# Three PSUM banks in turn for the edge products of a graph layer, with the sums issued one round later

## What is computed

```python
h = jnp.maximum(_layernorm(x, axis=-1), 0.0)          # x: 12500 x 64
e = jnp.concatenate([h[src], h[dst]], axis=1)         # 200000 edges, sorted by dst
m = jax.nn.relu(e @ W1 + b1) @ W2 + b2                # 128 hidden, 64 out
s = segment_sum(m, dst); cnt = segment_sum(1, dst)
x = x + s / jnp.maximum(cnt, 1.0)[:, None]
```

## Time and profile before

| | |
|---|---|
| median of 3 runs | 2825.12 us (2822.13 to 2827.91) |
| profiled execution | 2839.25 us, span 2837.4 us |
| mean granted TensorE clock | 0.749 of full speed |
| busy: PE / weight loads / DVE / ACT / POOL | 55% / 42% / 50% / 42% / 48% |

### The profile page before, as it was taken

The page is one execution under the profiler, slowest core; times in us unless marked ns, Lnnn a source line. Parts: engine busy times, 40 slices in busy tenths (PEclk is TensorE's granted clock), DMA queues, the critical chain, the costliest instruction groups (busy, mean ns, idle before and its releaser), DMA issues.

```text
span 2837.4 us, 26976 instructions
## 1 busy us (share of the span) xinstructions
PE 1548.3 (55%) x8249; PEld 1183.2 (42%) x8250; DVE 1428.9 (50%) x3051; ACT 1189.8 (42%) x2414; POOL 1372.7 (48%) x1460
## 2 busy tenths in 40 slices
PE   1656565566465564455544555455455545555556
PEld 0545353444344443344433444344344434434444
DVE  3554343343324665456655666456565556655421
ACT  1223343444314544345444454344344444444444
POOL 6345545445555445444554435545544554554553
PEclk6878777788787777677776777767776777776778
DMA  4532222222134656556565566556565665665541
GB/s 90 163 109 60 59 61 59 60 59 58 58 98 144 202 181 189 167 169 200 179 192 154 178 188 200 186 159 183 184 192 168 186 191 174 183 186 157 174 119 43
DMA packets 258990, 408.46 MB, mean 144 GB/s; under 512 B 45128, under 2 KB 118749, under 8 KB 258841
## 3 DMA queue, kind: packets, MB, share of 16 engines
q1 hardware_dynamic: 211845, 312.84, 35.7%
q0 software_dynamic: 46432, 93.61, 12.5%
q10 hardware_dynamic: 564, 0.23, 0.0%
HBM read 388.12 MB, written 18.38 MB: 143 GB/s over the span
## 4 chain that ended last, share of the span: by engine, by line
PE 48%; issue 36%; another core or an unknown queue 9%; DVE 6%; ACT 1%; DMA 0%; DVEq 0%; SPq 0%; ACTq 0%
PE z L1374 16%; PE bank L1401 12%; PE z L1386 10%; DVE g L1153 4%; PE bank L1419 2%; PE bank L1408 2%; PE z L1445 2%; PE bank L1430 1%; PE z L1461 1%; DVE rows_b L936 1%; PE bank L1268 1%; DVE norms L920 1%; PE z L1268 1%; ACT g L812 0%
## 5 line engine op out<-in xcount | busy, mean ns | idle before, releaser
L672 POOL DMA_INDIRECT g<-p_table,src_e x1403 | 1326.1, 945 | 1425.3 <-PE bank L1401 960.5
L1153 DVE SCALAR_TENSOR_TENSOR g<-z,norms,g 128x1024 bf16<-128x1024 f32 (+1 forms) x884 | 1019.1, 1214 | 43.5 <-issue 25.3
L812 ACT ACTIVATE g<-z 128x1024 f32<-128x1024 f32 x182 | 185.6, 1020 | 1468.0 <-remote 1153.5
L1100 DVE TENSOR_TENSOR acc<-acc,bank 65x128 f32 x191 | 54.2, 284 | 1201.0 <-remote 1069.7
L1374 PE MATMUL z<-work 128*128 128x128 f32 x1464 | 258.8, 348 | 514.2 <-issue 482.9
L1374 PE MATMUL z<-w,work 128*128 128x128 f32 x1438 | 251.9, 345 | 484.3 <-issue 443.8
L1374 PEld LDWEIGHTS z<-work 128*128 128x128 f32 x1464 | 240.3, 256 | 546.0 <-issue 541.7
L1374 PEld LDWEIGHTS z<-w,work 128*128 128x128 f32 x1438 | 234.4, 253 | 512.3 <-issue 509.3
L1401 PE MATMUL bank<-work,g 128*128 128x128 f32 x2902 | 423.4, 307 | 15.4 <-issue 15.1
L1401 PEld LDWEIGHTS bank<-work,g 128*128 128x128 f32 x2902 | 414.1, 227 | 16.8 <-issue 16.7
L1386 PE MATMUL z<-g,ident 128*128 128x512 f32 x726 | 350.8, 605 | 5.8 <-issue 5.7
(11 more groups left out here) (161 smaller groups left out, 1063.6 us busy)
## 6 DMA issues: line engine op xcount, KB each, us to landing
g<-tally_table SPq DMA_DIRECT2D x816, 256.0 KB
rel_q<-rel_table SPq DMA_DIRECT2D x46, 512.0 KB
rows_b<-rel_table SPq DMA_DIRECT2D x45, 512.0 KB
g<-p_table,src_e POOLq DMA_INDIRECT x1403
g<-tally_table SPq DMA_DIRECT2D x68, 128.0 KB
work<-q_table SPq DMA_DIRECT2D x96, 64.0 KB
w<-q_table SPq DMA_DIRECT2D x96, 64.0 KB
g<-p_table SPq DMA_DIRECT2D x12, 512.0 KB
```

The lines of the kernel that those rows point to most:

```text
L672: nc.gpsimd.indirect_dma_start(out=g[:, slot(n), j * HID:(j + 1) * HID], out_offset=None, in_=p_table, in_offset=bass.IndirectOffsetOnAxis ...
L812: nc.scalar.activation(rows_of_p(m), z[:, 0:HID * chunks_in(m)], ACT.Relu).then_inc(r_done, 1)
L1153: nc.vector.scalar_tensor_tensor(product[i % BUFFERS][:, 0:w], turned[:, 0:w], minus_q[:, d:d + 1], tally_row[i % BUFFERS][:, 0:w], ALU.ma ...
```

## The change

`z` becomes three banks used in turn by single quads (`z_of`), in place of a pair used by couples. Identity products and relus signal per quad, and `spread_q` takes one quad. To free a bank, both blocks of sums share one bank, and the first sums of a block wait until the block before is copied. TensorE's round becomes: the first quad's rows of Q of couple m+1, identity products of m, `times_w2`, sums of couple m-1, `dense(m)`, the second quad's rows of Q of couple m+1. The rounds of the other engines keep their order; ScalarE has two relus of 512 columns in place of one of 1024.

```diff
-        u_bank, turn_bank = bank[2:4], bank[4]
+        u_bank, turn_bank = [bank[2][:, 2 * WIN * k:2 * WIN * (k + 1)] for k in range(2)], bank[4]
+        z_of = [bank[0], bank[1], bank[3]]
...
+        def z_quad(n):
+            return z_of[(n - Q0) % len(z_of)][:, 0:HID * chunks_of(n)]
+
+        def quads_to(m):
+            return min(2 * m, QUADS - Q0)
...
             def relu(m):
-                act.wait_ge(z_done, m + 1)
-                nc.scalar.activation(rows_of_p(m), z[:, 0:HID * chunks_in(m)], ACT.Relu).then_inc(r_done, 1)
+                for n in couple(m):
+                    act.wait_ge(z_done, n - Q0 + 1)
+                    nc.scalar.activation(g[:, slot(n), 0:HID * chunks_of(n)], z_quad(n), ACT.Relu).then_inc(r_done, 1)
...
-            def spread_q(m):
-
+            def spread_q(n):
+
+                m, i = couple_of(n), GROUP[n]
                 pe.wait_ge(spread_done, parts_to(m + 1))
-                if m:
-                    pe.wait_ge(r_done, m)
+                if n - Q0 >= len(z_of):
+                    pe.wait_ge(r_done, n - Q0 + 1 - len(z_of))
...
             def sum_edges(m):
 
 
-                pe.wait_ge(r_done, m + 1)
+                pe.wait_ge(r_done, quads_to(m + 1))
                 if m < MEMBER_FROM:
                     pe.wait_ge(m_made, m + 1)
                 k = BLOCK[m]
+                if k and (m == 0 or BLOCK[m - 1] < k):
+                    pe.wait_ge(u_copied, k)
...
             def fast():
-                spread_q(0)
...
+                for n in couple(0):
+                    spread_q(n)
                 for m in range(COUPLES):
+                    if m + 1 < COUPLES:
+                        spread_q(couple(m + 1)[0])
                     add_rows(m)
                     if m >= 2 and m - 2 == BLOCK_END[BLOCK[m - 2]]:
                         times_w2(BLOCK[m - 2])
+                    if m:
+                        sum_edges(m - 1)
                     dense(m)
                     if m + 1 < COUPLES:
-                        spread_q(m + 1)
-                    sum_edges(m)
+                        for n in couple(m + 1)[1:]:
+                            spread_q(n)
                     for i in range(BATCHES):
                         if MEAN_AT[i] == m:
                             turn_batch(i)
+                sum_edges(COUPLES - 1)
```

More of the change, by code:

```diff
@@ L549, in load_window @@
                 if i >= WINDOWS:
-                    sp.wait_ge(zq_done, couple_of(GROUPS[i - WINDOWS][-1]) + 1)
+                    sp.wait_ge(zq_done, GROUPS[i - WINDOWS][-1] - Q0 + 1)
                 sp.dma_start(qw[k], q_table[bass.ds(first, WIN), :]).then_inc(window_in[k], 16)
@@ L1073, in spread_of @@
                 if m >= 2:
-                    dve.wait_ge(zq_done, m - 1)
+                    dve.wait_ge(zq_done, quads_to(m - 1))
                 dve.wait_ge(rows_there[m // 2 % 2], 16 * (m // 4 + 1))
@@ L1360, in _ @@
             pe.wait_ge(worst_done_i, 1)
-            def spread_q(m):
+            def spread_q(n):
+                m, i = couple_of(n), GROUP[n]
                 pe.wait_ge(spread_done, parts_to(m + 1))
-                if m:
-                    pe.wait_ge(r_done, m)
[L1368 to L1375, removed]
+                if n - Q0 >= len(z_of):
+                    pe.wait_ge(r_done, n - Q0 + 1 - len(z_of))
+                if n == GROUPS[i][0]:
+                    pe.wait_ge(window_in[i % WINDOWS], 16 * (i // WINDOWS + 1))
+                for c in range(chunks_of(n)):
+                    at = 512 * (n % 2) + 128 * c
+                    last = nc.tensor.matmul(z_quad(n)[:, 128 * c:128 * c + HID], spreads[m % 2][:, at:at + 128],
+                                            qw[i % WINDOWS], start=c == 0, stop=False)
                 last.then_inc(zq_done, 1)
@@ L1384, in add_rows @@
                 for n in couple(m):
[L1385 to L1388, removed]
+                    nc.tensor.matmul(z_quad(n), ident[:, :], g[:, slot(n), 0:HID * chunks_of(n)], start=False, stop=True)\
+                        .then_inc(z_done, 1)
             def sum_edges(m):
-                pe.wait_ge(r_done, m + 1)
+                pe.wait_ge(r_done, quads_to(m + 1))
                 if m < MEMBER_FROM:
```

## The result

The changed kernel takes 3264.36 us (median of 4 runs, 3258.61 to 3267.42), the kernel before 2823.94 beside it: ratio 1.1555, 95% interval 1.1533 to 1.1577. It is slower, and near the 3240 of the forecast. The profiled execution took 3262.66 for a span of 3260.7, so the sum of +415 is to be held against +423.3 of span. One of e3's four runs fell in the chip's slower state and is left out of e3's time.

What follows compares the result with a forecast made beforehand. No engine was busy over 55%; waits bound the kernel, one stall per gather burst. +460 us (product stage) and -45 (early rounds) gave +415, so 3254 profiled, 3240 us carried to the median; range 3000 to 3600.

Steps and rivals of the forecast that it cites:

- the sum of +415: Whole kernel: +460 us for the product stage less 45 for the early rounds, set against the profiled execution's 2839.25.
- The added loop: Product stage: sums, copy, members, spread, first quad's products, identity products and next sums run in series, 11.4 us per couple.
- the hold: TensorE results reported from about 8 us into a gather burst become known to other engines only at 22.8 us.
- Doubling these, 22.8 us per burst: Product stage: two couples of 11.4 us per burst would fit under the old 30.65 us period without the hold.
- The relus behind it, 1.2 us: ScalarE, product stage: relus of two quads, 0.62 us each, run only after the hold ends.
- Behind it, in series: After hold and relus: ScalarE 5.9, products 1.9, identity 3.4, counts 0.7, sums 2.0, POOL 0.3 us; period 38.2.
- 61 bursts of +7.55 = +460: Product stage: each burst's period grows from 30.65 to 38.2 us, +460 us over 61 bursts.
- Rounds up to 48, -45: First 22 bursts, where VectorE makes spreads and members: no closed loop, about -2 us each, at most -134 in all.
- First rival, TensorE itself stopped (3496): The hold stops TensorE's work itself; period 41.7 us, +11.0 for each of 61 bursts, 3496 us; chance 0.20.
- Second rival, a short hold (2500): The hold ends at 12.0 us or is gone; period 27.4 us, total 2500 us; faster case, chance 0.13.
- No change: ScalarE's members run early enough by overlooked slack; burst and hold still pin the period, 2825 us; chance 0.05.
- The 1.1 us that "stand open" at the relu: TensorE's gap per couple at the relu, meant to go: at most 2.2 us per burst, 183 us over 83 bursts.

Runs made afterwards that it cites:

- e3: Changed kernel with both quads' rows of Q put back behind the identity products, sums still one round late: 1865.54 us against 1845.65 for the kernel before.
- e5: Changed kernel, unaltered, on a chip without the hold: 2334.38 us against 1845.73 for the kernel before, ratio 1.2643.
- e4: Changed kernel with TensorE's old order of steps, three banks and per-quad signals kept, no hold: 1842.95 us against 1845.65 for the kernel before.
- e7: Kernel before with a wait put in by hand at ScalarE's relu, once per burst from round 49: 2570.4 us against 1848.55 without it.
- e12: Kernel of e4 with the wait put in by hand at ScalarE's relu, as in e7: 2480.77 us against 1849.43 for the kernel before without it.
- e8: Changed kernel with the wait put in by hand at ScalarE's copy, behind the relus: 3046.01 us against 1848.55 for the kernel before without it.
- e9: Changed kernel with ScalarE's spread one round earlier and the hand-made wait at the relus: 2725.63 us against 1848.55 for the kernel before without it.
- e6: Kernel before with POOL waiting for sums every second quad, so bursts of 8 gathers, not 16; no hold: 1837.64 us, ratio 0.9953.

## Why the prediction was right, point by point

- **The added loop (right; two terms too small).** e5 shows it with nothing else in the way. In the forecast it was 11.4 us a couple, and it is 13.7: the first quad's products take 2.08 and not 1.0, the identity products 2.98 and not 1.88, since "at full clock" does not hold behind the stops of 5 us in e5. The forecast used the loop at the low clock only behind the hold.
- **"Doubling these, 22.8 us per burst would still fit under 30.65".** It is 27.4. It fits under 30.65, but not under the 20 us that 16 gathers need, which is the bound once the hold is gone (e5).
- **The hold ends at 22.8 (right): 22.69.**
- **The relus behind it, 1.2 us (wrong).** "The results of both are held up to 22.8": the relus ran at 2220.96 and 2222.49, and VectorE saw W2's result at 2223.26, 11.9 us into the burst. Only the sums that ended at 2225.10 were kept back. This is the largest miss within a period.
- **Behind it, in series.** Copy, members and spread 5.9 (2234.10 to 2240.01: 5.9); products 1.9 (1.9); identity 3.4 (3.6); counts and W2 0.7 (0.9); sums 2.0 (2.05); to POOL 0.3 (0.3). Sum with 22.7: 37.3, forecast 38.2.
- **61 bursts of +7.55 = +460 (the sum +443, by two misses that offset each other).** Fifty-eight periods grew by 6.4, less than forecast. The four where POOL's lead shrinks grew by 69.5 together and not 30, since the two more couples cost a bare loop each: the forecast priced all bursts alike. That the total came within 17 us of +460 is partly luck.
- **Rounds up to 48, -45 (direction right): -21.4.** About 1.0 for each of 22 bursts. That the hold lasts 22.8 us "in most" is true of the product stage alone: below round 49 the 23 holds of the trace before end 12 to 23 us into their bursts, in the middle at 20.6, but for one in a burst of double length (33.9).
- **First rival, TensorE itself stopped (3496): falls.** By it the copy would come 4.7 us behind the release, 27.5 us into the burst, and a period would be 41.7; the copy comes at 22.69 and the period is 37.3. The Trainium skill (Perfetto Trace Analysis, Tensor Engine Instruction) says that a matmul's reported end is an estimate; the trace does not contradict this, and the 9.0 us between the sums' recorded end and the copy do not show by how much an estimate is off. What I drew from it, that the work itself would be left over, does not hold here.
- **Second rival, a short hold (2500): did not come about where the change was measured.** Its period of 27.4 is also what e5 has (twice 13.7), by coincidence: it was 12.0 of hold and 15.4 behind it. And its gain was reckoned against the old 30.65, which goes with the hold as well: without one the kernel before takes 1846, and the change is worse than with it (ratio 1.264).
- **No change: falls.**
- **Slips in the working.** The 1.1 us that "stand open" at the relu count one gap twice, since TensorE's 0.49 and the weight load's 0.70 in the earlier trace rows end together; the sum did not use them, and without a hold e4 gains 2.7 us in all. The lower end "36.0 (+329)" is 35.7 (+310) by its own terms. The "some 4 us" of work before the clock rose is 5.3 in that stall: TensorE starts at 722.64 and the clock is 0.54 from 727 to 728.

Of the signs, these came: periods near 38 (37.3), ScalarE idle before the copy and members, TensorE idle 5.1 us before the first quad's products, POOL's waits in the product stage at about 1160 us (1180 forecast), a granted clock of 0.70 there (0.73 before), and slightly shorter early rounds. One did not: behind the release no two relus come first, but the copy and the members at once, for the reason given above.

**Open.** Why one measurement has the hold and four chips do not is not settled. Bursts with idle time between them are not enough: e5's stand 27.3 us apart, and it has no hold. Nor is it settled what ends the hold. In the expectation of e7 I took it for the landing of the burst's last rows, and the traces speak against that. The gathers move on the DMA queue q0. In the burst of the earlier trace rows, from the last gather's end (2219.93) to 2221.25, and then over all queues up to the release (2221.25 to 2223.00), the trace before has

```profile
q0 software_dynamic: 34, 0.07, 18.8%
```
```profile
DMA packets 0, 0.00 MB, mean 0 GB/s; under 512 B 0, under 2 KB 0, under 8 KB 0
```

so the queue is empty for 1.8 us before ScalarE goes on. In another burst of the trace after the copy starts at 1039.36, and from 1039.40 to 1040.20 the queue still has

```profile
q0 software_dynamic: 2, 0.00, 0.1%
```

In nine bursts of each of the two traces, spread over the product stage, the queue's last packets came 1.0 to 4.0 us after the last gather's recorded end, and the hold ended 2.9 to 3.3 us after it every time. In the product stage the hold's end keeps its distance to that gather itself, not to its rows; in the early rounds even that distance varies (0.2 to 3.2 us). What passes from there to ScalarE's semaphore no trace shows. The waits drawn in e7 to e12 are therefore stand-ins of nearly the same length, not the real hold. Their place was read from a trace for e7 and e8; for e9 and e12 it was assumed. That e4's order would gain in the first measurement's conditions rests on e12's drawn hold; it was not run there. e6, which would have tried a hold with shorter bursts, was not run there either.

## What to carry to other kernels

Before moving an instruction ahead of another on one engine, write down the whole circle of who waits for whom across engines, with the order within each queue; if the move closes a circle, its length per round can be the new bound (e5). Where one engine stops in it, price that engine's work at the low clock too (13.7 us in e5, not 11.4). When a stall hides the true bound, price the change with the stall and without it, the rival's kernel before included. Per-quad signals and a third bank paid 90 us under a drawn hold (e12) and 2.7 us without one (e4), where the order that they allow costs 489 us (e5).

## What the runs showed of the hardware

- The same program took 2824 us in one measurement and 1846 to 1849 on four chips; TensorE's mean granted clock was 0.749 in the one and 0.905 to 0.920 in the others.
- In the trace after, results were visible 11.9 us into a burst, while the next one was kept to 22.7; in the trace before, one of 8.1 us was kept. The hold has no fixed start. In the product stage its end lies 2.8 to 3.3 us behind the last gather's recorded end in 120 of 121 bursts of the two traces.
- The rows of a burst's last gather are there 1.5 to 6.3 us after that gather's recorded end, in the middle 3.5 (the held relus of e7's product stage; 3.0 in the burst shown).
- TensorE's granted clock during ScalarE's 6 us behind the hold, and in TensorE's first 3 us after it, was 0.50, the 1.2 GHz level:

```profile
2234.00:2237.00 3.00, 0.00 (x0) 0.00 (x0) 0.00 (x0) 2.87 (x10) 0.00 (x0) 0.50 0.35 117
2240.00:2243.00 3.00, 2.94 (x10) 2.42 (x11) 0.00 (x0) 0.01 (x1) 0.00 (x0) 0.50 0.00 0
```

Columns as in the earlier trace rows. One quad's products took 2.08 us there, and 1.06 at 2224.94, at full clock. In the burst's first loop TensorE worked from 2217.14 on without a stop, and its granted clock was 0.50 up to 2221, 0.72 from 2221 to 2223, and 1.00 from 2223 to 2225.
